# Cross-attention with a feed-forward block on one core: all TensorE products but the probability products in two 64-row halves

## The reference

```python
def reference(x, ctx_1024, L0_xattn_Wq, L0_xattn_bq, L0_xattn_Wk, L0_xattn_bk, L0_xattn_Wv, L0_xattn_bv, L0_xattn_Wo, L0_xattn_bo, L0_ffn_W1, L0_ffn_b1, L0_ffn_W2, L0_ffn_b2):
...
        qh = _split_heads(q @ Wq.T + bq) / math.sqrt(HEAD_SIZE)
        kh = _split_heads(k @ Wk.T + bk)
        vh = _split_heads(v @ Wv.T + bv)
        scores = jnp.einsum('bhqd,bhkd->bhqk', qh, kh)
        attn = jax.nn.softmax(scores, axis=-1)
        ctx = jnp.einsum('bhqk,bhkd->bhqd', attn, vh)
        ctx = ctx.transpose(0, 2, 1, 3).reshape(q.shape[0], -1, SIZE)
        return ctx @ Wo.T + bo
...
        h1 = jnp.einsum('gmh,goh->gmo', xg, W1) + b1[:, None, :]
        h2 = jnp.einsum('gmo,gho->gmh', h1, W2) + b2[:, None, :]
        return h2.reshape(orig_shape)
    x = x + _L0_xattn_ref(_layernorm(x, axis=-1), ctx_1024, ctx_1024, L0_xattn_Wq, L0_xattn_bq, L0_xattn_Wk, L0_xattn_bk, L0_xattn_Wv, L0_xattn_bv, L0_xattn_Wo, L0_xattn_bo)
    x = x + _L0_ffn_ref(_layernorm(x, axis=-1), L0_ffn_W1, L0_ffn_b1, L0_ffn_W2, L0_ffn_b2)
    return x
```

## Time and profile before

| what | us |
|---|---|
| median of 3 runs | 620.83 |
| lowest and highest | 614.74, 621.23 |
| the profiled execution | 614.78 |
| its span, first to last instruction | 613.0 |
| granted clock of TensorE, mean | 0.989 |

### The profile page before, as it was taken

How to read it: one execution, slowest core, us unless ns; L and a number is a source line. 1 busy time by engine, 2 the same in 40 slices (tenths; PEclk the granted TensorE clock), 3 DMA queues, 4 the chain that set the end, 5 groups by cost and what they waited for, 6 DMA issues and landing times.

```text
span 613.0 us, 11485 instructions
## 1 busy us (share of the span) xinstructions
PE 584.0 (95%) x3380; PEld 296.0 (48%) x3380; DVE 458.9 (75%) x854; ACT 397.0 (65%) x746; POOL 221.2 (36%) x298
## 2 busy tenths in 40 slices
PE   7899989999999999999999999999999999889997
PEld 7545323545454544545444544445445454335457
DVE  5698787878888778787888777878788788786124
ACT  4217776776767586776667776676767766776741
POOL 5011028213660148212570138411481146313721
PEclk9969999999999999999999999999999999999999
DMA  8730333263224614254132823256042622260100
GB/s 291 186 93 2 86 90 105 54 215 115 81 62 131 213 40 140 54 194 133 45 95 55 264 61 117 47 161 189 8 137 53 208 54 76 66 208 2 69 21 34
DMA packets 34076, 65.23 MB, mean 106 GB/s; under 512 B 9778, under 2 KB 11642, under 8 KB 31994
## 3 DMA queue, kind: packets, MB, share of 16 engines
q1 hardware_dynamic: 34042, 64.81, 35.6%
HBM read 34.65 MB, written 4.44 MB: 64 GB/s over the span
## 4 chain that ended last, share of the span: by engine, by line
PE 83%; ACT 7%; issue 3%; POOL 2%; DVE 2%; DMA 1%; SPq 1%; ACTq 0%; DVEq 0%; POOLq 0%
PE st L449 20%; PE misc L471 20%; PE pv L463 18%; PE misc L549 11%; PE nat L439 8%; ACT probs L728 4%; PE misc L481 2%; ACT hi L748 1%; PE nat L430 1%; DMA bq_in<-bq 1%; PE misc L530 1%; ACT normedT_hi L741 1%; PE nat L471 1%; ACT normedT_hi L734 0%; POOL b_part L1185 0%
## 5 line engine op out<-in xcount | busy, mean ns | idle before, releaser
L896 DVE TENSOR_REDUCE neg_max<-nat 128x1 f32<-128x512 f32 x512 | 330.5, 679 | 78.9 <-PE nat L439 77.9
L728 ACT ACTIVATE probs<-st 128x512 f32<-128x512 f32 x505 | 283.3, 597 | 161.8 <-PE st L449 156.9
L449 PE MATMUL st<-qs,ks 64*128 64x512 f32 x505 | 200.9, 461 | 18.7 <-ACT probs L728 18.6
L439 PE MATMUL nat<-ks,qs 63*128 63x512 f32 x512 | 208.1, 471 | 1.9 <-DMA qs<-hi 1.1
L463 PE MATMUL pv<-probs,vs 128*32 128x512 f32 x1024 | 136.4, 605 | 0.0
L449 PEld LDWEIGHTS st<-qs,ks 64*128 64x128 f32 x505 | 80.5, 185 | 112.0 <-ACT probs L728 73.6
L439 PEld LDWEIGHTS nat<-ks,qs 63*128 63x128 f32 x512 | 83.4, 187 | 11.8 <-DVE neg_max L896 7.0
L549 PE MATMUL misc<-w_in 128*128 128x256 f32 x256 | 80.7, 411 | 0.0
L1147 POOL TENSOR_TENSOR pair_ctx<-pair_ctx,inv_sum 128x512 f32<-128x512 f32 x15 | 19.1, 1276 | 118.7 <-DMA inv_sum<-inv_dram 118.7
L549 PEld LDWEIGHTS misc<-w_in 128*128 128x128 f32 x256 | 40.6, 189 | 42.9 <-issue 35.5
L463 PEld LDWEIGHTS pv<-probs,vs 128*32 128x32 f32 x1024 | 20.1, 108 | 38.7 <-issue 35.8
(11 more groups left out here) (168 smaller groups left out, 803.5 us busy)
## 6 DMA issues: line engine op xcount, KB each, us to landing
w_in<-w SPq DMA_DIRECT2D x8, 1024.0 KB
w_in<-w2T SPq DMA_DIRECT2D x8, 1024.0 KB
ks<-hi SPq DMA_DIRECT2D x64, 128.0 KB, 2.4
qs<-hi SPq DMA_DIRECT2D x64, 128.0 KB, 2.5
x_in<-x SPq DMA_DIRECT2D x8, 512.0 KB, 3.4
ctx_in<-ctxT SPq DMA_DIRECT2D x8, 512.0 KB, 4.3
ks<-lo SPq DMA_DIRECT2D x32, 128.0 KB, 2.4
qs<-lo SPq DMA_DIRECT2D x32, 128.0 KB, 2.6
```

Source lines behind the costliest of these rows:

```text
L439: mm(nat_of(n)[:, :], qs[rows, 2 * g + jj, c * P:(c + 1) * P], ks[rows, 2 * g + jj, :], start=True, stop=True).then_inc(nat_done, 1)
L449: mm(st_of(u, prep)[:, :], ks[rows, 2 * g + jj, kc * P:(kc + 1) * P], qs[rows, 2 * g + jj, :], start=True, stop=True).then_inc(st_done, 1)
L728: act.activation(probs[kc % 2][:, j, :], st_of(u, prep)[:, :], ACT.Exp).then_inc(exp_done, 1)
L896: dve.tensor_reduce(neg_max[:, g % 2, at:at + 1], nat_of(n)[:, :], AX.X, ALU.max, negate=True).then_inc(max_done, 1)
```

## The change

All products that had 128 rows, but pv and b2sum, become two products of 64 rows. The halves of one product go, one after the other in time, to the same bank; at any moment the two row halves of the array work on the two banks. A job runs in two phases: in phase 0 rows 0 to 63 write `misc[0]` and rows 64 to 127 `misc[1]`, in phase 1 the other way round, after a wait (`crossed`) for both halves of phase 0. So every job of two outputs takes both `misc` banks at once. V moves from units 0 to 4 to units 32 to 36, K to 4 to 8, xT to 12 and 13, Q to 16 to 20, b2sum to 22 ahead of its pv, yT to 39 and 40; all of W21 stands at 51 to 63, and in the lead for turn 0. Copies out of the banks move with them on ScalarE and VectorE. Jobs follow each unit, not each second unit, and a pv comes after the third unit of four. The maxima's transpose takes a place in the ring of three `nat` banks, as two halves around that unit's `st` and `nat`, at units 4, 20, 36 and 52; `neg_max` is widened to 128 columns for it. SP's and GpSimd's orders are changed. The diff, cut; the old `jobs` and the old small job functions that go are in the listing above.

```diff
+ATTN_SPLIT = 58
 ST_HEADS = ((0, 0), (0, 1), (1, 0), (1, 1))
 NAT_HEADS = ((0, 1), (0, 0), (1, 1), (1, 0))
 STACKS = 2 * len(SLOTS) * 16
 QK_ORDER = ((1, 0), (1, 1), (0, 0), (0, 1))
 QK_BANKS = (0, 1, 0, 1)
 FIRST_BANKS = (0, 1, 4, 5)
+RING = UNITS + QUADS
+STEPS = ((0, 0), (0, 1), (1, 0), (1, 1))
+K_UNITS = (4, 5, 7, 8)
+XT_UNITS = (12, 13)
+Q_UNITS = (16, 17, 19, 20)
+B2_UNIT = 22
+WO_UNITS = (24, 25, 27, 28)
+V_UNITS = (32, 33, 35, 36)
+YT_UNITS = (39, 40)
 Z_UNITS = (44, 45, 47, 48)
+W21_UNITS = ({51: (0, 1), 52: (2, 3), 53: (4, 5), 55: (6, 7)},
+             {56: (0,), 57: (1, 2), 59: (3, 4), 60: (5,), 61: (6,), 63: (7,)})
+HALF_UNITS = (9, 10, 21, 22)
...
-        neg_max = sb("neg_max", [P, 2, 16])
+        neg_max = sb("neg_max", [P, 2, P])
...
+        def at_nat(n):
+            return n + n // 16
+        def at_maxT(g):
+            return 17 * g + 16
+        def ring(at):
+            return nat_bank[at % NATS]
...
+        def maxT_of(b, u, prep):
+            n = u + LEAD
+            if n % 16 or (n > UNITS and not prep):
+                return None
+            return (b, n // 16 - 1) if n <= UNITS else (b + 1, (n - UNITS) // 16 - 1)
...
             def turn(b, post, prep, load):
                 if post:
+                    stack_quad(b, 3)
                     gather_sums(b - 1, 1)
-                    stack_quad(b, 3)
                 store_max(b, 1)
+                if load:
+                    wait_apart(sp, norm_ready[0], 4 * (b + 2))
+                    load_x(b + 2)
                 if post:
                     save_inverse(b - 1, 1)
                     spread_inverse(b - 1, 1)
                 if prep:
                     stack_quad(b + 1, 0)
                 store_max(b, 2)
+                if prep:
+                    stack_quad(b + 1, 1)
+                gather_sums(b, 0)
                 if load:
-                    wait_apart(sp, norm_ready[0], 4 * (b + 2))
-                    load_x(b + 2)
                     wait_apart(sp, v_done, 2 * (b + 2))
                     wait_apart(sp, qk_done, 4 * (b + 2))
                     load_ctx(b + 2)
-                if prep:
-                    stack_quad(b + 1, 1)
-                gather_sums(b, 0)
                 store_max(b, 3)
                 save_inverse(b, 0)
+                spread_inverse(b, 0)
+                if prep:
+                    stack_quad(b + 1, 2)
                 if post:
                     store_out(b - 1, 0)
-                spread_inverse(b, 0)
-                if post:
                     store_out(b - 1, 1)
                 load_y(b)
                 if prep:
-                    stack_quad(b + 1, 2)
                     store_max(b + 1, 0)
...
+                at = at_nat(n)
+                wait(pe, max_done, RING * b + {0: -1, 1: 0, 2: -2}.get(at, at - 2))
+                mm(ring(at)[:, :], qs[rows, 2 * g + jj, c * P:(c + 1) * P], ks[rows, 2 * g + jj, :],
                    start=True, stop=True).then_inc(nat_done, 1)
+            def maxT(b, g, rows):
+                at = at_maxT(g)
+                wait_apart(pe, max_done, RING * b + at)
+                cols = slice(rows.start, rows.stop)
+                return nc.tensor.transpose(ring(at)[:, cols],
+                                           neg_max[rows, g % 2, :], ident[rows, cols])
...
+            TILES = (slice(0, HALF), slice(HALF, P))
+            TERMS = ((0, 0), (1, 0), (0, 1))
+            def order(phase):
+                return (0, 1) if phase == 0 else (1, 0)
+            def crossed(job, count, phase):
+                if phase == 1:
+                    wait_apart(pe, half_done[job], count)
...
+            def transposed(phase, job, done):
+                for c in range(C):
+                    for t in order(phase):
+                        f, rows = t ^ phase, TILES[t]
+                        last = nc.tensor.transpose(misc[f][:, c * P + HALF * t:c * P + HALF * t + HALF],
+                                                   normed[rows, c, f * P:(f + 1) * P], ident[rows, rows])
+                        if c == C - 1:
+                            last.then_inc(done if phase else half_done[job], 1)
...
+            def qk_step(which, phase, f):
+                src, w = ((normedT_hi, normedT_lo), WQ) if which == 0 else ((ctx_hi, ctx_lo), WK)
+                for n, (i, j) in enumerate(TERMS):
+                    for t in order(phase):
+                        m, rows = t ^ phase, TILES[t]
+                        last = mm(misc[m][:, :], (w_hi, w_lo)[i][rows, w, f, m * P:(m + 1) * P], src[j][rows, f, :],
+                                  start=(phase == 0 and f == 0 and n == 0), stop=(phase == 1 and f == F - 1 and n == 2))
+                        if f == F - 1 and n == 2:
+                            last.then_inc(qk_done if phase else half_done["qk"[which]], 1)
+            def rows_step(job, lefts, rights, phase, s, done):
+                for f in range(F):
+                    for n, (i, j) in enumerate(TERMS):
+                        for t in order(phase):
+                            half, rows = t ^ phase, TILES[t]
+                            c = 2 * half + s
+                            last = mm(misc[half][:, s * D:(s + 1) * D], lefts[i][rows, f, c * P:(c + 1) * P],
+                                      rights[j](rows, f), start=(phase == 0 and s == 0 and f == 0 and n == 0),
+                                      stop=(phase == 1 and s == 1 and f == F - 1 and n == 2), skip_group_check=True)
+                            if s == 1 and f == F - 1 and n == 2:
+                                last.then_inc(done if phase else half_done[job], 1)
...
+            def w21_step(phase, o):
+                for t in order(phase):
+                    f, rows = t ^ phase, TILES[t]
+                    last = mm(misc[f][:, 0:D], w1_in[rows, o, f * P:(f + 1) * P], w2_in[rows, o, :],
+                              start=(phase == 0 and o == 0), stop=(phase == 1 and o == OC - 1))
+                    if o == OC - 1:
+                        last.then_inc(w21_done if phase else half_done["w21"], 1)
             def jobs(b, u, post, prep):
+                if prep and u in K_UNITS:
+                    phase, f = STEPS[K_UNITS.index(u)]
+                    if u == K_UNITS[0]:
+                        wait(pe, w21_ready, b if post else 1)
+                        wait(pe, v_ready, 2 * b + 2)
+                        wait(pe, ctx_ready, b + 2)
+                    if f == 0:
+                        crossed("k", 2 * b + 2, phase)
+                    qk_step(1, phase, f)
+                if prep and u in XT_UNITS:
+                    phase = XT_UNITS.index(u)
+                    if phase == 0:
+                        wait(pe, lo_ready, 4 * b + 6)
+                        wait_apart(pe, norm_ready[0], 4 * b + 8)
+                    crossed("xT", 2 * b + 2, phase)
+                    transposed(phase, "xT", xT_done)
+                if prep and u in Q_UNITS:
+                    phase, f = STEPS[Q_UNITS.index(u)]
+                    if u == Q_UNITS[0]:
+                        wait(pe, xT_ready, 2 * b + 4)
+                    if f == 0:
+                        crossed("q", 2 * b + 2, phase)
+                    qk_step(0, phase, f)
+                if post and u in WO_UNITS:
+                    phase, half = STEPS[WO_UNITS.index(u)]
+                    if u == WO_UNITS[0]:
+                        wait(pe, b2_ready, b)
+                        wait(pe, lo_ready, 4 * b + 8 if prep else 0)
+                        wait(pe, attn_ready, 2 * b)
+                    if half == 0:
+                        crossed("wo", 2 * b, phase)
+                    rows_step("wo", (attnT_hi, attnT_lo), weight(WO), phase, half, wo_done)
+                if prep and u in V_UNITS:
+                    phase, half = STEPS[V_UNITS.index(u)]
+                    if u == V_UNITS[0]:
+                        wait(pe, y_ready, 2 * b if post else 0)
+                        wait(pe, lo_ready, 4 * b + 8)
+                    if half == 0:
+                        crossed("v", 2 * b + 2, phase)
+                    rows_step("v", (ctx_hi, ctx_lo), weight(WV), phase, half, v_done)
+                if post and u in YT_UNITS:
+                    phase = YT_UNITS.index(u)
+                    if phase == 0:
+                        wait(pe, v_ready, 2 * b + 4 if prep else 0)
+                        wait(pe, y_ready, 2 * b)
+                        wait_apart(pe, norm_ready[1], 4 * b)
+                    crossed("yT", 2 * b, phase)
+                    transposed(phase, "yT", yT_done)
+                if post and u in Z_UNITS:
+                    phase, half = STEPS[Z_UNITS.index(u)]
+                    if u == Z_UNITS[0]:
+                        wait(pe, yT_ready, 2 * b)
                         wait(pe, w21_ready, b)
+                    if half == 0:
+                        crossed("z", 2 * b, phase)
```

(73 more changed lines are left out.)

221 lines of the change are left out of this document (25 added, 196 removed).

## The result

The changed kernel takes 665.9 us (median, 660.6 to 681.7) against 621.0 us (614.7 to 624.0) for the kernel before on the same chip: 1.074 times as long, 95% interval 1.063 to 1.084. In a second comparison it took 670.4 us (661.6 to 680.7) against 621.7, 1.069 times as long (1.058 to 1.079). Ratios with their intervals compare the fast executions alone, medians are of all. The forecast was 654 in a range of 612 to 700, with a chance of 0.77 for slower.

A forecast was written before the change was run, and what follows sets the result against it. TensorE was taken as the bound (95% busy). A steady turn of 61 us work and 13.7 of waits was put at 75; 614.8 + 6 x 4.3 + 3.5 + 7 = 651, plus 3, gave 654 us, range 612 to 700.

The forecast's parts named there:

- steps 1, 2 and 3: Steady turn: TensorE's work 61 us, waits for emptied job banks 10.8, waits of the row maximum's transposes 1.6.
- xT to Q: Handoff after unit 15: Q's first product waits for the xT copies, 2.43 us against 0.68 of TensorE work, wait 1.75.
- The transposes of the maxima: At units 4, 20, 36 and 52 they hold TensorE's queue for the previous unit's row maximum: 1.6 us a turn.
- TensorE's own work: Products, loads and transposes of a steady turn when nothing waits: 61 us, with shape changes worth close to 10 gone.
- ScalarE's bursts: normalise at units 6 and 7 delays exp 8 by 0.7 us, W21's copies at unit 0 cost 0.6: 1.3 a turn.
- Step 5: Moved DMAs cost nothing; attn_split at unit 18 comes 3 us late in the last turn, 1 us in steady turns, swallowed.
- step 6: Ends of the kernel: lead +3.5 us from 16 W21 steps instead of 8, turn 0 about 0, last turn +7.
- the 3 us added from the spread of before: Half of the 6 us by which the median of runs before exceeded the profiled execution, raising 651 to 654.
- A: Rival: shape changes decide, waits under 7 us a turn, turn 65, kernel about 584 us; chance 0.17.
- B: Rival: gains and waits cancel, steady turn 69, waits 7 to 9 us, kernel 609 to 621 us; chance 0.06.
- C: Rival: halves don't overlap in 256-column or fp32 products, 7 us x 7 turns more, about 700 us; chance 0.10.
- the second bound of the fp32 case: W21's fp32 products: if two row halves did not overlap in fp32, another 6.9 us.

The follow-up runs named there:

- no_handoffs_chain: no_handoffs with the reciprocal moved from unit 11 to 9 and the split of the divided context from unit 18 to behind exp(21): 617.1 us.
- no_handoffs: Changed kernel with copies out of the job banks reading a fixed tile from the second turn on and TensorE not waiting for them; values not the reference's: 641.1 us.
- after_again: The changed kernel once more, with no edit, for a second profile: 670.4 us.
- combined: chain_earlier and late_max together, plus the b2 row summed inside z instead of its own product and copy: 612.3 us, 0.979 times the kernel before.
- retimed: Changed kernel with the copies out of the job banks issued one or two units earlier, both banks' copies one behind the other: 646.8 us, 1.038 times before.
- late_max: Changed kernel with three of the four pairs of maxT transposes a turn issued one unit later on TensorE: 660.5 us, 1.064 times before.
- filled: Changed kernel with 43 dummy 64-row products a turn in front of the jobs' waits, results overwritten: 667.0 us.
- chain_earlier: retimed with the reciprocal moved from unit 11 to 9 and the split of the divided context from ahead of exp(19) to behind exp(21): 630.4 us.

## Why the prediction was right, and where it was off

**The turn (steps 1, 2 and 3).** 75 forecast, 75.0 to 75.2 measured at the full clock, in both profiles. Term by term, the forecast wait and the one listed in turn 5: xT to Q 1.75 and 1.7; Q to b2sum 1.8 and 1.5; b2sum to output 0.8 and 0.7; output to V 1.7 and 1.4; V to yT 1.15 and 1.0; yT to z 1.35 and 1.2; z to W21 1.15 and 0.9; K to xT 1.1 and 1.0: 10.8 and 9.4. The list counts from the modelled end of the product before, so it comes out short. From starts the terms are better still. The last `st` before Q starts at 447.48 and Q's first product at 449.54. Less the 0.23 at which such products repeat, that is 1.83, against 1.75 forecast. In the same order the eight are 1.8, 1.7, 0.9, 1.6, 1.3, 1.3, 1.1 and 1.2: 11.0 for 10.8. The transposes of the maxima are 1.6 forecast, 1.3 listed and 1.8 from starts.

TensorE's own work was forecast at 61, 1.3 of it for loads that nothing hides after a wait. Its parts, from the distances in the same turn: 16 blocks of four units at 2.12, 8 steps of K and Q at 0.71, 12 of V, output and z at 0.71, 4 of transposes at 0.38, 16 of W21 at 0.445, b2sum 0.65, the maxima's transposes about 2: 59.4. With 11.0 and 1.8 of waits that is 72.2; the 2.8 left of 75.0 stand against 2.6 forecast for ScalarE's bursts and those loads, which weren't measured one by one. So the sum is right because its parts are, and not by luck.

**What the turn's sum could not say.** That the waits are not additive. Taking the handoffs (10.8 forecast) and the blocked ScalarE away together gave 5.1 to 6.3 us a turn (no_handoffs_chain), and taking only the handoffs away gave 3.4 (71.6 in turn 5, with 3.4 us at 1.2 GHz in it), because the wait of attn_split came in their place. Step 5 had named it ("at unit 18 ... it comes 3 us too late; ScalarE then blocks exp. In steady turns it is 1 us late, which the waits swallow"): 1.0 to 1.4 us in the changed kernel, 3.0 to 3.6 where the waits had gone. The expectation for no_handoffs left it out.

**The ends (step 6).** Lead forecast +3.5: 46.1 to 47.5 in five profiles of the variants against 42.4, so +3.6 to +5.0. But both profiles of the changed kernel have 58.7 and 58.1, with the same instructions in the lead. After_again's lead in two stretches:

```profile
0.00:26.10 26.10, 20.87 (x111) 17.84 (x111) 16.54 (x30) 10.43 (x17) 9.18 (x17) 0.93 0.73 225
26.10:58.10 32.00, 31.66 (x53) 13.78 (x54) 14.93 (x25) 1.60 (x3) 2.35 (x1) 0.50 0.31 87
```

From 26.1 on TensorE is busy to the full and yet at 1.2 GHz. Four of the nine profiles with this lead have such a stretch, from about 26 to 70 us; in the other five it lasts from about 45 to 59. Turn 0: forecast 0, +1.5 measured, with 12.3 us at 1.2 GHz where before had 5.4. Last turn with the tail: forecast +7, measured 92.1 for 83.5, +8.6, with 17 us at 1.2 GHz in it.

**What the prediction left out** is the granted clock, which no step has: every term is priced as at 2.4 GHz. Against its own profiled execution the forecast was +36.3 us (651 for 614.8), and after_again shows +59.3. Of the 23 us between, 12.2 are the lead, 7.7 turns 1 to 6 (33.5 for 25.8), 1.5 turn 0 and 1.6 the end. The 7.7 lie in turns 2 and 3, which are 5.6 and 2.6 us longer than turns 4 and 5, with 13.7 and 6.8 us at 1.2 GHz in them. The nine recorded executions of the changed kernel say the same: from 660.6 us at a mean granted clock of 0.961 to 681.7 at 0.922 they lie close to one line, 5.1 us for each hundredth of the clock. Drawn on to the 0.989 of the profile before, it gives 647. That is an estimate beyond the range measured, but it puts the sum of 651 within some 4 us of what the change costs at the clock of before, and the rest above it on the low clock. That 654 comes within 12 us of the median is in part luck: the 3 us added from the spread of before stand in for a loss that the working doesn't name, and how much of it an execution has varies, 660.6 to 681.7 us.

**The rivals.** A (the shape changes decide) set its bound at under 7 us of waits a turn: 11.2 were listed. Combined is under that bound with 2.4, and even so its turn is 68.4 and not A's 65. B needed a steady turn of 69: no. C (halves don't overlap): no, 0.12 for a pair of 256 columns, 0.24 of 512, and a step of W21, two fp32 pieces in both halves, 0.445 where 0.43 was forecast; the second bound of the fp32 case, 6.9 us, is refuted.

**The moved DMAs (step 5).** Costed at nothing, and no DMA stands in TensorE's list of waits in turn 5. The old order of the DMAs wasn't run.

## What to carry to other kernels

When a change makes a job take all the buffers that two jobs shared by turns, write down each handoff as the time of the copies in their order, less what the producer can do meanwhile, at the units where the copies really stand in their queues. Here that sum came out at 75 of 75 us. But don't subtract those waits again when they are to be cured: find what ends next after each. Here it was a chain of DMAs whose length didn't shrink with the turn, and an engine that waited for it with urgent work behind. And give the schedule its say before the idea is given up: the half-products were 7% slower than before with copies one by one at fixed units, and 1 to 3% faster with copies paired and moved, the transposes later and the b2 row inside z.

## What the runs showed of the hardware

**The granted clock falls in a kernel whose TensorE pauses for less than 2 us at a time** (the longest idle times listed in turn 2 are 1.8 and 1.7 us). Before, it was at 2.4 GHz from turn 1 to the end. In the changed kernel (turn 2) it went to 1.2 GHz at 217.3, in unit 17, again at 227.5 and at 251.4. The rows are the 5.3 us before the first fall, then the first and the second stretch:

```profile
212.00:217.30 5.30, 3.64 (x34) 1.89 (x34) 4.38 (x8) 3.26 (x6) 0.00 (x0) 1.00 0.17 39
217.30:220.70 3.40, 3.40 (x18) 1.07 (x14) 1.38 (x2) 1.46 (x3) 1.27 (x1) 0.51 0.96 326
227.50:234.30 6.80, 6.27 (x44) 3.88 (x40) 2.67 (x4) 3.16 (x6) 0.00 (x0) 0.50 0.23 52
```

Ahead of the fall TensorE had been busy 3.64 of 5.30 us, the wait of xT to Q in it. In the low stretches pairs of 256-column halves repeat at 0.21 to 0.22 us for 0.12. Turns 4 and 5 hold the same waits and no fall, so the waits make it possible and don't decide when. In turns 2 to 5 it fell in 2 of 4 in both profiles of the changed kernel, 3 of 4 in retimed and late_max, 4 of 4 in no_handoffs, and in none in filled, chain_earlier, combined and no_handoffs_chain; filled differs from the changed kernel by nothing but the dummies. The places are few: in turns 1 to 6 of all ten profiles every fall but those in unit 42 came in units 16, 17, 21 and 22. In the changed kernel Q's and b2sum's waits stand there, in no_handoffs and retimed the `st`s behind the blocked ScalarE.

The Trainium skill, "TensorE: Matmul & The Clock Gate", section "Part 1: The HAM clock gate (the "warmup" mystery)", says that the clock is set by how busy TensorE has been recently and that the start of the full clock varies from run to run. The steady turns agree with the first: with TensorE 73.4 of 76.0 us busy no turn of filled had a fall. The long stretch in four of the nine leads doesn't fit it, with TensorE busy for 31.66 of 32.00 us at 1.2 GHz. The second is seen in these leads, which are back at the full clock at 58 to 60 us in five profiles and at 70 to 72 in four. What exactly lets the clock fall, and what holds it down in those leads, stays open here.

**Loads of two row halves run side by side in the jobs**: in after_again the pairs of loads for 256-column products start at 461.21, 461.33 and 461.45, 0.12 us apart, the distance at which single 128-row products follow each other in the earlier trace rows.
